# The first stage of a fused attention and mixture-of-experts kernel in another order: loads on one queue, tiles turned in three passes, gate in passes 4 to 7, token rows scattered before padding rows

## The reference, cut to what matters

```python
x = L0_attn_x                                   # (4, 512, 512) float32
xn = layernorm(x)
out = x + attention(xn) + ffn(xn)

def ffn(x):                                     # 7 routed experts, 3 for each token, one shared expert
    output = (silu(x @ Ws1) * (x @ Wsg)) @ Ws2
    p = softmax(x @ gate_w + gate_b)
    idx = top_k(p + biases, 3)
    w = p[idx] / sum(p[idx])
    for e in range(7):
        w_e = sum(w * (idx == e))
        output += (silu(x @ W1[e]) * (x @ Wg[e])) @ W2[e] * w_e
    return output
```

## Time and profile before

| | |
|---|---|
| median of 3 runs | 1473.83 us (1473.40 to 1474.04) |
| profiled execution | 1469.24 us, span 1467.5 us |
| mean granted TensorE clock | 0.969 |
| busy share: PE, DVE, ACT, POOL | 90%, 53%, 46%, 48% |
| PE idle by its waits, 0 to 420 us | 59 us in six groups |

### The profile page before, as it was taken

How to read it: one execution, slowest core, us unless ns; L and a number is a source line. 1 busy time by engine, 2 the same in 40 slices (tenths; PEclk the granted TensorE clock), 3 DMA queues, 4 the chain that set the end, 5 groups by cost and what they waited for, 6 DMA issues and landing times.

```text
span 1467.5 us, 20562 instructions
## 1 busy us (share of the span) xinstructions
PE 1323.1 (90%) x6233; PEld 1062.6 (72%) x6233; DVE 776.3 (53%) x1481; ACT 674.7 (46%) x1207; POOL 700.0 (48%) x684
## 2 busy tenths in 40 slices
PE   3899479999999999999986998889889899999997
PEld 2677368788888888888775776667667677777776
DVE  4634022222222222222245788878777888888887
ACT  3222122222222222222236776666666676777774
POOL 3206714991320032000003578888888876566564
PEclk9899689999999999999989999999999999999999
DMA  7416843663331133111050122333242231001002
GB/s 262 143 45 232 278 142 115 188 188 95 97 106 59 59 95 98 58 59 59 29 178 1 42 37 54 61 72 56 44 85 50 45 49 23 14 1 28 1 30 86
DMA packets 80630, 123.32 MB, mean 84 GB/s; under 512 B 18640, under 2 KB 26960, under 8 KB 80528
## 3 DMA queue, kind: packets, MB, share of 16 engines
q1 hardware_dynamic: 47232, 56.13, 12.9%
q0 software_dynamic: 11312, 27.23, 8.3%
q10 hardware_dynamic: 21984, 38.65, 8.0%
HBM read 78.60 MB, written 43.25 MB: 83 GB/s over the span
## 4 chain that ended last, share of the span: by engine, by line
PE 55%; POOL 20%; issue 10%; ACT 6%; DVE 5%; another core or an unknown queue 2%; ACTq 1%; DMA 0%; POOLq 0%; DVEq 0%; SPq 0%
PE bank L47 50%; POOL moe L570 6%; POOL p_store L559 2%; PE bank L1416 2%; POOL rot L552 2%; DVE store_b L1258 2%; ACT p_store L839 2%; POOL sum_b L592 2%; POOL sum_b L590 2%; POOL rot_sin L549 2%; PE bank L1355 2%; POOL sum_a L589 1%; POOL store_b L601 1%; DVE p_store L1300 1%
## 5 line engine op out<-in xcount | busy, mean ns | idle before, releaser
L47 PE MATMUL bank<-slots,x_turned 128*128 x1296 | 324.8, 399 | 0.9 <-issue 0.9
L47 PE MATMUL bank<-store_b,store_a 128*128 128x512 f32 (+1 forms) x1536 | 313.1, 359 | 2.9 <-DVE store_b L1251 1.6
L47 PEld LDWEIGHTS bank<-store_b,store_a 128*128 128x128 f32 x1536 | 258.5, 189 | 58.5 <-issue 9.2
L47 PEld LDWEIGHTS bank<-slots,x_turned 128*128 128x128 f32 x1296 | 239.2, 188 | 55.0 <-issue 2.2
L47 PE MATMUL bank<-store_b 128*128 128x512 f32 x768 | 205.2, 412 | 58.1 <-DVE store_b L1251 43.4
L919 DVE TENSOR_TENSOR hid_t<-bank,hid_t 128x512 fp32r<-128x512 f32 x70 | 48.4, 692 | 367.0 <-ACT hid_t L650 334.9
L47 PE MATMUL bank<-slots,hid_t 128*128 (+1 forms) x840 | 215.6, 407 | 24.4 <-DVE hid_t L919 21.6
L47 PEld LDWEIGHTS bank<-store_b 128*128 128x128 f32 x768 | 144.7, 196 | 113.4 <-issue 85.1
L47 PEld LDWEIGHTS bank<-slots,hid_t 128*128 128x128 f32 x840 | 158.1, 194 | 58.0 <-DVE hid_t L919 19.8
L1273 DVE SCALAR_TENSOR_TENSOR acc<-bank,inv_store,acc 128x512 f32<-128x512 f32 x256 | 186.0, 748 | 12.6 <-PE bank L47 0.5
L530 POOL CAST slots<-staging 128x512 f32 x72 | 44.2, 613 | 223.8 <-PE bank L47 223.8
(11 more groups left out here) (201 smaller groups left out, 1786.4 us busy)
## 6 DMA issues: line engine op xcount, KB each, us to landing
sorted_y<-y_store ACTq DMA_DIRECT2D x54, 256.0 KB
rows<-sorted_x ACTq DMA_DIRECT2D x51, 260.0 KB, 2.7
staging<-in_w SPq DMA_DIRECT2D x48, 256.0 KB
staging<-in_wg SPq DMA_DIRECT2D x24, 256.0 KB
xn_rows<-rows_a SPq DMA_DIRECT2D x16, 256.0 KB, 3.2
shared_y<-y_store ACTq DMA_DIRECT2D x16, 256.0 KB
rows_a<-xn_rows SPq DMA_DIRECT2D x16, 256.0 KB
raw<-in_wot SPq DMA_DIRECT2D x16, 256.0 KB, 4.3
```

The source lines that it names most:

```text
L47: made = pe.matmul(out, a, b, start=first and n == 0, stop=last and n == len(pairs) - 1)
```

## The change

It leaves the passes from 8 on, the scatter's 55 indirect DMAs and all the attention as they are, and rearranges the first stage:

- ACT issues only the loads of tiles 0 to 3. Tiles 4 and 5, the gate's weights and biases, the table and the seven zero blocks go to SP's queue, the last five of these behind most or all of the loads. ACT runs one small silu on its way (`warm`).
- Tiles 0 to 3 are turned in four PSUM banks in place of two; tiles 4 to 15 in passes 0 to 2.
- POOL makes the low parts of chunks 0 to 3 before `rstd_of(2)`, then a pair after each `rstd_of`.
- Logits are made in passes 1 to 3, the gate's maths is drawn in passes 3 to 6, `count_rows` is at the end of pass 4.
- POOL scatters the token rows first and the padding rows last, with no wait between.

```diff
-        TURNS = {0: ((4,), (5,)), 1: ((6, 7), (8, 9)), 2: ((10, 11), (12, 13)), 3: ((14, 15), ())}
+        TURNS = {0: ((4, 5), (6, 7)), 1: ((8, 9), (10, 11)), 2: ((12, 13), (14, 15))}
-            return banks[4 + n % 2]
+            return banks[4 + n % (2 if n >= FIRST_TURNS else 4)]
...
-            for k in range(3):
+            for k in range(NS):
                 load_shared(k)
-            for k in range(3, CH):
+            for t in range(FIRST_TURNS, XR):
+                sp.dma_start(rows_a[:, t, 0:D], x_t[:, t, :]).then_inc(on[f"x_in{t}"], 16)
+            load_shared(NS)
+            sp.wait_ge(on["pad_made"], 1)
+            sp.dma_start(gw_raw[:, :, 0:NE], gate_w.rearrange("(c p) e -> p c e", p=P)).then_inc(on["gate_in"], 16)
+            load_shared(NS + 1)
+            spill(0)
+            spill(1)
+            load_shared(NS + 2)
+            spill(2)
+            load_x(XR)
+            load_shared(NS + 3)
+            spill(3)
+            load_x(XR + 1)
+            for k in range(NS + 4, CH):
                 load_shared(k)
-                if 4 <= k < 4 + XR:
-                    spill(k - 4)
-                if 6 <= k:
-                    load_x(k)
+                spill(k - 4)
+                load_x(k)
...
+            for n in range(NE):
+                sp.dma_start(sorted_x[(NR - NE + 1 + n) * P:(NR - NE + 2 + n) * P, :], rows_a[:, XR, :]).then_inc(
+                    on["zeros_in"], 16)
...
             pool.wait_ge(on["zeros_in"], 16 * NE)
-            pool.wait_ge(on["padding_made"], 1)
-            for e in range(NE):
-                pool.indirect_dma_start(sorted_x, bass.IndirectOffsetOnAxis(ap=padding[:, e:e + 1], axis=0),
-                                        rows_a[:, XR, :], None).then_inc(on["padded"], 16)
-            pool.wait_ge(on["padded"], 16 * NE)
             pool.wait_ge(on["share_made"], 1)
             pool.wait_ge(on["placed"], 1)
...
+            pool.wait_ge(on["padding_made"], 1)
+            for e in range(NE):
+                pool.indirect_dma_start(sorted_x, bass.IndirectOffsetOnAxis(ap=padding[:, e:e + 1], axis=0),
+                                        rows_a[:, XR, :], None).then_inc(on["padded"], 16)
...
-            for t in range(XR):
+            for t in range(FIRST_TURNS):
                 act.dma_start(rows_a[:, t, 0:D], x_t[:, t, :]).then_inc(on[f"x_in{t}"], 16)
...
+            act.activation(warm[:], neg_half[:, 0:1], ACT.Silu)
...
+                if b < 2:
+                    for g in (2 * b + 4, 2 * b + 5):
+                        statistics(g)
+                        normalise(2 * g)
+                        normalise(2 * g + 1)
```

More of the change, by code:

```diff
@@ L114, in program @@
             neg_half = tile(ctx, "neg_half", [P, NT])
+            warm = tile(ctx, "warm", [P, 1])
             gw_raw = tile(ctx, "gw_raw", [P, DC, 8])
@@ L476, in pool_program @@
             rstd_of(1)
[L477 to L480, removed]
+            for k in range(DC):
                 shared_low(k)
[L482 to L490, removed]
+            for g in range(2, 6):
+                rstd_of(g)
+                shared_low(2 * g)
+                shared_low(2 * g + 1)
             rstd_of(6)
@@ L679, in load_first @@
                               ).then_inc(on[f"staged{n % NS}"], 16)
[L681 to L684, removed]
             split_high(0, slot1)
             split_high(1, slot1)
+            split_high(2, slot1)
             turn_high(0)
-            split_high(2, slot1)
-            turn_high(1)
             split_high(3, slot1)
[L691 to L694, removed]
+            for t in range(1, FIRST_TURNS):
+                turn_high(t)
+            for n in range(4, 8):
                 split_high(n, slot1)
[L696 to L699, removed]
             for b in range(NBK):
@@ L1120, in gate_maths, with work @@
                 step(dve.tensor_copy(block_tab[:, :, 1], block_f[:, 1]), "tables_made")
+            def work(steps):
+                for _ in range(steps):
+                    next(gate, None)
+            gate = gate_maths()
             statistics(0)
@@ L1125, in vector_program @@
             normalise(1)
+            normalise(2)
             turn_low(0)
-            normalise(2)
-            turn_low(1)
             normalise(3)
+            for t in range(1, FIRST_TURNS):
+                turn_low(t)
             statistics(2)
-            turn_low(2)
-            turn_low(3)
             normalise(4)
@@ L1135, in vector_program @@
             statistics(3)
[L1136 to L1139, removed]
+            normalise(6)
+            normalise(7)
             for b in range(NBK):
@@ L1145, in vector_program @@
                     turn_low(t)
-                if b in (5, 6, 7):
-                    for _ in range(10 if b == 5 else 6 if b == 7 else 0):
-                        next(gate, None)
+                if b == 4:
+                    work(8)
+                if b == 5:
+                    work(7)
+                if b == 6:
+                    work(7)
                 multiply(b)
@@ L1152, in vector_program @@
                 if b == 0:
[L1153 to L1168, removed]
+                    dve.wait_ge(on["gw_high"], 1)
+                    dve.tensor_tensor(gw[:, :, 8:16], gw_raw[:], gw[:, :, 0:8].bitcast(F32), ALU.subtract).then_inc(
+                        on["gw_low"], 1)
+                if b < 2:
[3 more added lines that the diff above has]
+                        normalise(2 * g + 1)
+                if b == 3:
+                    work(12)
                 if b == 4:
-                    for _ in range(10):
-                        next(gate, None)
+                    work(6)
                 if b == 5:
-                    for _ in range(8):
-                        next(gate, None)
+                    work(10)
                 if b == 6:
[L1176 to L1180, removed]
+                    work(100)
                 if FIRST_JOB < b <= FIRST_JOB + CH // 2:
@@ L1466, in tensor_program @@
                     turn_rows(t)
[L1467 to L1469 removed]
+                if b == 2:
+                    logits_back(0)
+                    logits(1)
+                if b == 3:
+                    logits_back(2)
                     logits(3)
[L1471 to L1472 removed]
                 gated(b)
@@ L1475, in tensor_program @@
                     turn_rows(t)
-                if 1 <= b <= 3:
-                    logits(b - 1)
-                if b == 4:
+                if b == 1:
+                    logits(0)
+                if b == 2:
+                    logits_back(1)
+                    logits(2)
+                if b == 3:
                     logits_back(3)
```

45 lines of the change are left out of this document (28 added, 17 removed).

## The result

The changed kernel takes 1481.35 us (median of 20 runs, 1477.81 to 1485.15), the kernel before 1475.34 us beside it (20 runs, 1471.42 to 1479.29). The ratio is 1.0038, 95% interval 1.0027 to 1.0048: **slower by 6 us**, 0.4%. The prediction was 1470 us, 4 us less than the 1473.83 us it started from, so the time went the other way, and it lies 0.35 us above the upper end of the range, 1481. The profiled execution took 1483.88 us with a span of 1482.1, against 1469.24 and 1467.5. So the pair of profiles differs by 14.6 us, more than the medians do: the profiled execution of before took less than any of its 20 runs here. The pair is read for places and mechanisms, not for the sum.

The account below looks back on a forecast made before the run. PE was taken as nearly full except at the start and in a hole at 138 to 196 us. 1469.24 - 4 (lead) + 0 (hole) = 1465.2 profiled; runs stand 4.6 us above, so 1470 us, range 1430 to 1481.

Parts of the forecast that it names:

- up(0): At the start: four low parts in a row on POOL let it begin at 16.5 us, a lead of 5.8 us.
- gated(0): At the start: after tile 7's load, statistics and two low parts, it begins at 27.1 us, a lead of 5.9 us.
- the cost that I set against the Trainium skill: Start, SP's single load queue: waits in order delay tile 7; without that cost the lead would be about 7 us.
- up(2) and the lead: Passes 0 and 1: begins at 53 to 55 us, not 57.16; DVE gives part back, leaving a lead of 4 us.
- the sum of DVE's steps: Passes 0 and 1: DVE's turns, statistics and normalise steps after multiply(0) at 32.2 take 15.6 us.
- Gate and scatter: Gate in passes 3 to 6 costs 0; places at some 100 us, padding until 174, blocks read by 178.
- The hole: same length, I take 0: PE's stretch from 138 to 196 us, where 40 us are lost: taken as unchanged, 0 us.
- +13: Bound on added loss, in us, if the hole lasts over the whole 75 us of the scatter.
- rival 2: The hole grows with the padding at its end: +5 to +13 less 4, 1475 to 1483 us; chance 0.20.
- The scatter isn't late in either case: Blocks read by 178 us, before PE's turn_block(0), at 184 if the hole is gone; earlier scatter worth nothing by itself.
- Rival 1: The hole goes during the scatter: 1430 us, half gone 1450; chance 0.20 whole, 0.13 partly.
- Rival 4: Token scatters beside DVE's gate maths: 0.4 us, or 1473 us if descriptors are held back; chance 0.04.

Follow-up runs that it names:

- e5: The kernel before with bounds checks on its loaded block numbers and job limits; in a set with the hole, 1480.34 us, 1.0048 against before.
- e6: The changed kernel with bounds checks on its loaded block numbers and job limits; in a set with the hole, 1487.87 us, 1.0103 against before.
- e15: The changed kernel with bounds checks, padding DMAs first and a wait for them before the token rows; with the hole, 1483.24 us, 1.0091 against before.
- e2: The kernel before with bounds checks, token rows scattered first, padding last, no wait between; without the hole, 1446.05 us, 1.0051 against before.
- e9: Repeat of e2 in a later set, the kernel before with bounds checks and padding last; without the hole, 1446.33 us, 1.0049 against before.
- e14: The changed kernel with bounds checks and a 0.5 us POOL memset after each tile's scatter; with the hole in its set, 1442.66 us, 0.9819 against before.
- e3: The changed kernel with bounds checks on its loaded block numbers and job limits; in a set without the hole, 1437.83 us, 0.9988 against before.
- e1: The kernel before with bounds checks on its loaded block numbers and job limits; in a set without the hole, 1448.44 us, 1.0073 against before.
- e8: The changed kernel with bounds checks, SP's plain stores replacing POOL's 55 indirect DMAs, padding not written; set with the hole, 1439.17 us, 0.9766 against before.

## Why the prediction was wrong, point by point

- **up(0)**: forecast at 16.5, came at 17.29. Four low parts in a row, as forecast, on the right chain.
- **gated(0)**: forecast at 27.1, came at 30.32, after 6.90 us of waiting for POOL's low parts. The chain was the right one, tile 7's load, its statistics, `rstd_of(3)` and two low parts, but the load was priced too low: the statistics ran at 25.68, still waiting for the DMA, where I had tile 7 landed by 22.5. The order on SP's queue made little of that: tile 6's load was issued at 18.45 where I had 17.4, and tile 7's at 19.84. What took long was its landing, 5.8 us after the issue. The trace of before had that price, a load issued at 23.18 whose statistics ran at 28.58, 5.4 us; I took some 3, as for the writes of the earlier trace rows. Tiles 6 and 7 are loaded on SP's queue in both kernels, so the cost that I set against the Trainium skill, "DMA: Bandwidth & Descriptors", section "Issuing engines are not separate DMA queues", by which several issuing engines save only issue time, is tested by no run here.
- **up(2) and the lead**: forecast at 53 to 55 and 4 us; came at 55.95, and in pass 8 `turn_hidden` is 2.3 us ahead (121.69 against 123.96). `multiply(0)` came at 35.73 in place of 32.2, behind the late `gated(0)`; from it to PE's next wait, at 50.30, the sum of DVE's steps was right to a microsecond (14.6 us for 15.6). The mechanism holds; the 4 is a 2 (1.7 in the pair without the hole).
- **Gate and scatter**: places forecast at 100, made at 102.29; first token scatter right behind, at 103.53; last padding DMA at 175.75 (forecast 174), blocks read at 178.59 (forecast 178).
- **"The hole: same length, I take 0"** is the step that failed. It costs 52.8 us in place of 40.0, which with a lead of 2.3 in place of 4 turns the forecast gain of 4 us into a loss of 10.5 at `turn_block(0)` in the profiles. In the medians the loss is 6 us; with the same lead that would be some 8 us more in the hole, an estimate. The +12.8 is just the bound that I had written for a hole that lasts all through the scatter, +13, and this was rival 2. What I had for the 0 was that the number of DMAs in a row might set the hole's start, and that the seven padding DMAs only changed sides. The start did come after about as many DMAs, 13 to 16 in the five traces below, but the loss didn't follow from that. The hole is bounded here by the first "remote" wait (the time of its row less its wait) and the end of POOL's last indirect DMA:

| | hole, us | after the first indirect DMA | us lost in it | share |
|---|---|---|---|---|
| before | 139.6 to 191.9, 52.3 | 24.5 | 40.0 | 0.77 |
| `e5`, the same order | 139.3 to 191.0, 51.7 | 24.5 | 46.1 | 0.89 |
| changed | 120.4 to 176.7, 56.3 | 16.8 | 52.8 | 0.94 |
| `e6`, the same order | 123.6 to 176.3, 52.8 | 20.2 | 52.8 | 1.00 |
| `e15`, early gate, padding first | 122.1 to 177.6, 55.5 | 19.7 | 47.0 | 0.85 |

  The start is known to some 3 us only, as such a wait holds an engine's usual idle time too, and the first row that was released behind the last DMA came 0.2 to 5 us after it. So in every order the hole begins 17 to 25 us after POOL's first indirect DMA and ends with the last or a few us later. In the changed order it starts 4 to 8 us sooner behind the first DMA and is 1 to 4 us longer, but for the most part it is *denser*: PE loses 94 to 100% of it, where it lost 77 to 89% in the old one. I had taken a fixed loss of 40 us; the place that a hole may fill and the share that is lost in it were two terms, and both moved. Each row is one execution, and the two of the old order differ by 6.1 us among themselves, so the size of the difference is uncertain.
- **Rival 2 gave the right size, for a reason that isn't shown.** I tied the growth to the padding DMAs at the end of the chain. In the table the shares go by the padding's place and not by the gate's: 0.77 to 0.89 in the three kernels with the padding first, early gate or late, and 0.94 and 1.00 with it last. The time of `e15` says the opposite, its ratio is nearly that of `e6`. A run of `e2` or `e9` with the hole would have helped to settle it; both fell into sets without. Shown is that the changed order loses more in the hole and that POOL's pace decides on whether there is one (`e14`). Why it loses more isn't shown: beside the padding, the passes, the reloads and ACT's loads stand at other points of the scatter, and no run separates them.
- **"The scatter isn't late in either case"** was right for the changed kernel (without the hole `turn_block(0)` at 184.71, forecast 184) and wrong for the one before: without the hole it waits 9.2 us for rows that are read at 193.03. Only because the hole held PE up by 40 us was the scatter of before early enough. So in a set without the hole the change is worth 10.6 us, and with it, it costs 6 to 7.5.
- **Rival 1, the hole goes**: it did, but for a reason outside the kernel, and for both kernels. My "1430 if it goes" is 1437.83 in `e3`, whose check of bounds costs some 0.5 to 0.7%.
- **Rival 4**: token scatters beside the gate's maths took 1.22 us for the first and 0.96 for the others; no lock was seen. The Trainium skill, "SBUF — State Buffer", section "SBUF: two separate sides", has a DMA of GpSimd's queue go from some 620 to some 3100 ns beside a DVE `tensor_copy`; that is the time of the whole DMA, where I had taken it for the issue. No issue of the changed kernel took over 1.22 us.

**What stays open**: why PE's work is seen late while POOL's indirect DMAs follow one another every 1.27 us. The trace gives most of PE's idle time to "issue" or to DVE's `hid_low`, and the longest waits of ACT and DVE to "remote". PE's matmuls start 2.1 us apart or not at all in 153 to 168 us of the changed kernel, so it isn't only their signals that are late, as I had written: PE itself hardly advances. That the engines were short of instructions is a rival that no run tests; the queues that bring instructions moved nothing from 124 to 196 us of the changed kernel, where `e3` had two such blocks between 144 and 172; but where PE hardly advances it needs few, so this tells nothing either way. No run settles which part of the chip holds it.

## What to carry to other kernels

Where a stretch is lost for a reason that the trace can't name, don't forecast that it keeps its length: look at what begins it and what ends it, and move both with the change. Let a long train of indirect DMAs on POOL run only as fast as its consumer needs it: here half a microsecond of idle work a tile cost up to half a per cent where there was no stall, and where there was one of some 50 us it was gone. And measure a change at several times: here its sign was another where a stall, which is there at one time and not at another, hid the wait that the change removes.

## What the hardware showed that I had not expected

- The same kernel took 1439.7 us and 1469.98 us on one chip in two sets, with runs within 0.5% of their median in each. The difference of 30 us fits a stall of some 40 us (before, `e5`) that is in one set and not in the other, less the 9 us for which PE waits for sorted rows where there is no stall (`e1`).
- In that stall PE makes four matmuls in 16 us (160 to 176) and in `e6` none, while only POOL's queue moves data, at 200 GB/s and 51.3% of the DMA engines (210 and 53.9% in `e6`); with SP's plain stores (`e8`) PE is full at 291 GB/s.
- The step from 4.0 to 4.5 us a tile (three indirect DMAs) is enough to end it: the changed kernel has one wait of 48.64 us, `e14` none, beside `e15` in the same set, which lost 47.0 us.
- PE's granted clock is 0.50 in 160 to 180 us of the changed kernel and 0.77 in 180 to 200, behind the stall; where PE ran through (`e14`) it is 1.00 in 138 to 180.
